# One-hot codes of a head's chosen tokens: 64 comparisons with a constant over four token tiles, where eight comparisons of two tensors stood, and the gathering put in the same order

## The reference

```python
q = jnp.einsum('bsd,hd->bhs', x, Wq)
keys = jnp.einsum('bsd,hd->bhs', x, Wk)
v = jnp.einsum('bsd,ed->bse', x, Wv).reshape(B, S, H, dv).transpose(0, 2, 1, 3)
k_idx = jnp.argsort(keys, axis=-1)
k_sorted = jnp.take_along_axis(keys, k_idx, axis=-1)
v_sorted = jnp.take_along_axis(v, k_idx[..., None], axis=2)
top_keys, bot_keys = k_sorted[:, :, -k:], k_sorted[:, :, :k]      # k = 32
top_vals, bot_vals = v_sorted[:, :, -k:, :], v_sorted[:, :, :k, :]
attn_top = jax.nn.softmax(q[..., None] * top_keys[:, :, None, :], axis=-1)
attn_bot = jax.nn.softmax(q[..., None] * bot_keys[:, :, None, :], axis=-1)
...
out = q_pos * out_top + (1.0 - q_pos) * out_bot
```

## Time and profile before

| | |
|---|---|
| median of 3 runs | 1083.82 us (1082.76 to 1086.74) |
| the profiled execution | 1083.07 us |
| its span, first to last instruction | 1080.8 us |
| mean granted TensorE clock | 0.924 of full speed |
| busy: TensorE, VectorE, ScalarE, GpSimd | 903.8, 880.1, 620.6, 457.1 us |
| the one-hot operations (L1950) | 16 of them, 40.5 us in all |
| the attention of the second block | about 733 to 966 us of the span |

### The profile page before, as it was taken

How to read it: one execution, slowest core, us unless ns; L and a number is a source line. 1 busy time by engine, 2 the same in 40 slices (tenths; PEclk the granted TensorE clock), 3 DMA queues, 4 the chain that set the end, 5 groups by cost and what they waited for, 6 DMA issues and landing times. The chain is left out here.

```text
span 1080.8 us, 16981 instructions
## 1 busy us (share of the span) xinstructions
PE 903.8 (84%) x5454; PEld 603.9 (56%) x5454; DVE 880.1 (81%) x1724; ACT 620.6 (57%) x1331; POOL 457.1 (42%) x439
## 2 busy tenths in 40 slices
PE   5568999999999999999889969985288558747996
PEld 4346777777777777777667725463222442234554
DVE  6868999999999999988899787669979787665443
ACT  2568777777778787777677522215268508614111
POOL 2337666777675454554445562112500410007332
PEclk9889999999999999999999989998679769956999
DMA  5013433334433222321222310001000000021001
GB/s 195 25 59 109 133 135 122 123 104 124 134 128 113 69 79 81 125 89 60 78 85 73 139 58 1 2 30 29 2 0 1 1 1 1 1 78 55 1 1 40
DMA packets 44031, 72.44 MB, mean 67 GB/s; under 512 B 4595, under 2 KB 20979, under 8 KB 43305
## 3 DMA queue, kind: packets, MB, share of 16 engines
q1 hardware_dynamic: 34728, 58.79, 17.1%
q10 hardware_dynamic: 9216, 12.59, 3.1%
HBM read 56.81 MB, written 13.76 MB: 65 GB/s over the span
## 5 line engine op out<-in xcount | busy, mean ns | idle before, releaser
L477 PE MATMUL bank<-hTs,wA 128*128 128x512 bf16 x768 | 178.2, 380 | 0.8 <-DVE u L1573 0.8
L1573 DVE SCALAR_TENSOR_TENSOR u<-bank,chn,u 128x511 f32<-128x511 f32 (+2 forms) x192 | 142.9, 744 | 9.1 <-ACT u L1071 5.6
L2103 POOL TENSOR_TENSOR xbuf<-xbuf,dec 128x384 f32<-128x384 f32 x64 | 53.4, 834 | 208.1 <-ACT xbuf L1079 168.8
L548 PE MATMUL bank<-wB,yb 128*128 128x256 f32 x512 | 121.2, 380 | 0.7 <-DVE acc L1529 0.7
L477 PEld LDWEIGHTS bank<-hTs,wA 128*128 128x128 bf16 x768 | 75.1, 98 | 83.4 <-issue 3.9
L548 PEld LDWEIGHTS bank<-wB,yb 128*128 128x128 f32 x512 | 92.5, 190 | 11.1 <-issue 1.1
L477 PE MATMUL bank<-hTs,w13s 128*128 128x512 bf16 x372 | 92.5, 396 | 7.1 <-DVE uc L1801 3.8
L2163 POOL TENSOR_TENSOR hfl<-hf 128x512 bf16<-128x512 f32 x44 | 46.0, 1044 | 120.3 <-DVE hf L1811 66.6
L2113 POOL TENSOR_TENSOR yb<-yv,gs 128x512 f32<-128x512 f32 x64 | 81.7, 1276 | 15.5 <-DVE yv L1600 15.3
L621 PE MATMUL bank<-Mm,xbuf 128*128 128x128 f32 x512 | 69.8, 279 | 21.0 <-DVE yv L1600 18.6
L1089 ACT ACTIVATE rel<-csb,cs 128x128 f32<-128x128 f32 x256 | 82.4, 415 | 0.0
(11 more groups left out here) (247 smaller groups left out, 2099.7 us busy)
## 6 DMA issues: line engine op xcount, KB each, us to landing
csb<-csd SPq DMA_DIRECT2D x64, 256.0 KB, 3.4
wA<-in_win SPq DMA_DIRECT2D x32, 256.0 KB, 4.3
wAd<-wA ACTq DMA_DIRECT2D x32, 256.0 KB, 4.2
wA<-wAd SPq DMA_DIRECT2D x32, 256.0 KB, 3.7
wB<-in_wob SPq DMA_DIRECT2D x8, 512.0 KB, 5.8
wBd<-wB ACTq DMA_DIRECT2D x32, 128.0 KB, 4.3
wB<-wBd SPq DMA_DIRECT2D x8, 512.0 KB, 5.4
CB<-in_wbc SPq DMA_DIRECT2D x2, 1024.0 KB, 9.4
```

The lines of the kernel that those rows point to most:

```text
L477: last = nc.tensor.matmul(out, wpart(a, kt), hpart(c, kt), start=n == 0, stop=n == 5)
L548: last = nc.tensor.matmul(out[:, 0:D], yb[:, HG * (k % 2) + m, t * P:(t + 1) * P], wB[:, k % 2, m, :], start=m == 0, stop=m == HG - 1)
L1573: nc.vector.scalar_tensor_tensor(out=u[:, n % 2, d:S], in0=bank[0][:, 0:S - d], scalar=chn[:, hid, 3 - d:4 - d], in1=u[:, n % 2, d:S], op0 ...
```

## The change

The tensor `iotak` and the operation that makes it are gone. The eight operations of each batch that compared two tensors become 64, one per side and place. Each compares all four token tiles of `cdT`, 512 elements a partition, with one number given in the instruction, and writes runs of four heads (8 bytes) into `OH`, with a distance of 256 bytes from one run to the next. The elements written are as many as before (32,768 a partition and batch). `a_oh` is raised once per side, not once per tile. The gathering matmuls are the same 256, but run side by side, then by group, then by token tile; a bank is full when the second side's matmuls of its four groups are done. `add_heads` of the second batch stands behind the first side.

```diff
-        iotak = sb("iotak", [P, 2, K, QG], bf16)
@@ TensorE, gathering
-                    for t in range(TB):
-                        pe.wait_ge(q["a_oh"], TB * b + t + 1)
+                    for side in range(2):
+                        pe.wait_ge(q["a_oh"], 2 * b + side + 1)
                         for n in range(NQ // 4):
                             for g4 in range(4):
-                                for side in range(2):
-                                    o = (g4 * 2 + side) * 48
+                                g = 4 * n + g4
+                                o = (g4 * 2 + side) * 48
+                                for t in range(TB):
                                     last = nc.tensor.matmul(
-                                        bank[n][:, o:o + 48], OH[:, t, side, 4 * n + g4, :],
-                                        PV[:, t, :, 16 * n + 4 * g4:16 * n + 4 * g4 + 4, :],
-                                        start=t == 0 and o == 0, stop=t == TB - 1, skip_group_check=True)
-                            if t == TB - 1:
+                                        bank[n][:, o:o + 48], OH[:, t, side, g, :],
+                                        PV[:, t, :, 4 * g:4 * g + 4, :],
+                                        start=o == 0 and t == 0, stop=t == TB - 1, skip_group_check=True)
+                            if side:
                                 last.then_inc(q["a_vw"], 1)
@@ VectorE
-                nc.vector.tensor_copy(iotak[:].rearrange("p s k h -> p (s k) h"),
-                                      cst[:, C_IOTA:C_IOTA + 2 * K].unsqueeze(2).to_broadcast([P, 2 * K, QG]))
...
-                    for t in range(TB):
-                        for side in range(2):
-                            last = nc.vector.tensor_tensor(
-                                OH[:, t, side].rearrange("p g (k h) -> p g k h", h=QG),
-                                cdT[:, t, :].rearrange("p (g h) -> p g h", h=QG).unsqueeze(2).to_broadcast([P, NQ, K, QG]),
-                                iotak[:, side].unsqueeze(1).to_broadcast([P, NQ, K, QG]), ALU.is_equal)
+                    for side in range(2):
+                        for k in range(K):
+                            last = nc.vector.tensor_scalar(OH[:, :, side, :, QG * k:QG * (k + 1)],
+                                                           cdT[:].rearrange("p t (g h) -> p t g h", h=QG),
+                                                           float(side * K + k + 1), None, ALU.is_equal)
                         last.then_inc(q["a_oh"], 1)
-                        if b and t == 0:
+                        if b and side == 0:
                             add_heads(b - 1)
```

## The result

| | median us | range | n | before beside it, us (n) | ratio to before, 95% interval |
|---|---|---|---|---|---|
| changed | 1077.79 | 1074.89 to 1080.38 | 6 | 1083.43 (6) | 0.993 [0.9912, 0.9949] |
| changed, second measurement | 1075.53 | 1073.71 to 1076.88 | 4 | 1084.32 (12) | 0.9905 [0.9886, 0.9925] |
| changed, third measurement | 1073.2 | 1070.89 to 1078.56 | 6 | 1085.0 (10) | 0.9892 [0.9861, 0.9923] |

In the third measurement one execution of before took 1152.75 us at a granted clock of 0.801 and is not counted.

A forecast was written before the change was run, and what follows sets the result against it. VectorE's one-hot codes were taken to bound the gathering and sums, in the second batch only behind `add_heads`. Gains of 3.5 + 2.0 + 0.1 = 5.6 us from 1083.07 gave 1077.5, median 1078 us; range 1075 to 1089.

The forecast's parts named there:

- The price of a comparison: On VectorE, each new 512-element comparison follows the last after 0.20 us; 0.33 or 0.60 were the alternatives.
- Rival 2: VectorE's fixed part per operation is not overlapped: pitch 0.29 us, 4.5 us slower, 1088 us; chance 0.04.
- First batch: Codes end at 779.05 instead of 783.44; sums end 4.2 or 2.8 us earlier, 3.5 taken.
- full-clock tail: From last code to end of sums, 4.5 us if TensorE gathers the second side at full clock, 5.9 at half.
- Second batch: Side 0 ends at 871.85, `add_heads` at 874.5; sums end 2.7 or 1.3 us earlier, 2.0 taken.
- the failed step: Second batch: GpSimd's last four operations alternate with one VectorE comparison each, until 868.05.
- Rival 1: VectorE handles two elements a step, not four: pitch 0.33 us, about 11 us slower, 1095 us; chance 0.13.
- Rival 3: The stream of short comparisons keeps GpSimd out until it ends, in both batches: about 1086.5 us; chance 0.05.
- The tail and the clock: Tails of 4.5 or 5.9 us behind the last codes; clock shifts in the loops behind worth 1.2 us either way.
- The sum: Gains of 3.5 us in the first batch, 2.0 in the second and 0.1 for `iotak`: 5.6 us.
- likeliest case: Whole kernel at pitch 0.20 us with turns between VectorE and GpSimd: 1075 to 1081 us; chance 0.75.

The follow-up runs named there:

- e2: Changed kernel with the copied codes `cdT` in fp32 instead of bf16: 1095.06 us, ratio to before 1.0088.
- e3: Kernel before, in its old tile-by-tile order, with 256 constant comparisons of 128 elements a batch: 1103.08 us, ratio to before 1.0169.
- e9: Changed kernel with each comparison of the second batch's side 0 cut in two of 256 elements: 1082.72 us in a single execution, before 1083.07.
- after_third: The changed kernel without edit, measured and profiled a third time: 1073.2 us, ratio to before 0.9892.
- e5: Changed kernel with the tensor `iotak` and the operation that fills it put back, unused: 1075.26 us, ratio to before 0.9909.
- e6: Changed kernel, VectorE waiting ahead of the second batch's eleventh comparison for the first of GpSimd's last four pieces: 1079.66 us, ratio to before 0.994.
- e8: Changed kernel with the ninth comparison of the second batch's side 0 reading its codes from PSUM: 1074.63 us in a single execution, before 1083.07.
- after_again: The changed kernel without edit, measured and profiled a second time: 1075.53 us, ratio to before 0.9905.
- e4: Changed kernel with the first batch's first 20 comparisons and all 32 of the second batch's side 0 reading codes from PSUM: 1074.31 us, ratio to before 0.9892.
- e7: Changed kernel with 20 comparisons of the first batch and 27 of the second batch's side 0 reading PSUM: 1072.33 us, ratio to before 0.9897.

## Why the prediction was right, and where it was not

**The price of a comparison: right.** 0.20 us was taken between 0.20, 0.33 and 0.60; 0.202 was measured. The reason holds as well (e2, e3, e9). Rival 2 is out: the pitch is 0.202 with a duration of 0.302, so the fixed part is overlapped. The Trainium skill, VectorE: DVE Perf Modes, section The DRAIN you can't avoid, which I cited for this rival, adds itself that a next operation which isn't held starts earlier; here the next one does start 0.1 us before the one ahead is over.

**First batch: the size right, the path partly by chance.** Forecast 4.2 us at the full-clock tail and 2.8 at the other, 3.5 taken; 3.9 measured from `VW` to the sums. In the runs in which VectorE reached the codes as before (22.64 us: after_third, e5, e6, e8, e9), the codes took 16.43 us, forecast 16.6 at most, and the gain is 25.80 - 21.47 = 4.3. In after_third:

```profile
765.12 16.43 DVE L1948 TENSOR_SCALAR OH<-cdT 128x512 bf16<-128x512 bf16 x64
```

In the first profile VectorE reached the codes 2.9 us earlier against its own start than before, so six of its comparisons, not three, lay beside GpSimd's operations, at 1.4 us each. What differs ahead of it is the granted clock:

```profile
724.10:737.80 13.70, 13.70 (x56) 12.16 (x54) 10.82 (x40) 0.97 (x5) 0.00 (x0) 0.50 0.18 59
```

It was 0.50 through this window in the changed kernel's profile, and 0.88 in that of before and of e5. Over the window from 715 to 745 us it is 0.77 in the five profiles with 19.6 to 20.05 us from `VW` to the codes (changed, after_again, e2, e4, e7) and 0.94 in the nine with 22.63 to 22.65. TensorE, ScalarE and with them GpSimd came later against VectorE (GpSimd's first operation of the attention starts 8.06 us behind `VW`, not 5.43), VectorE's search for keys met less of GpSimd (the two operations that write `code`, L1911 before, took 3.40 us there and 1.26 here), and its codes met more. From `VW` to the sums it hardly matters: 44.55 against 44.11 us. I call this chance and not a result of the change, because both versions occur in the same kernel (after_again and after_third) and e6 broke the only pattern.

**Second batch: the failed step.** "Then GpSimd's four last with one of VectorE behind each: 862.25 + 4 x 1.45 = 868.05", so that side 0 ends at 871.85. The prediction took the turns for a law. They hold when GpSimd is at work as VectorE's stream comes. Here the stream was running when GpSimd came, at 862.57, and its operation, 1.3 us of work, lasted 5.3 us, since it waited until the stream was over. Side 0 ended at 866.7, not 871.85, and `add_heads` at 871.4, not 874.5. Some of what this won was lost again: GpSimd's late pieces stood beside `x_sb` (2.00 us, forecast 1.24) and one comparison of side 1 (1.3 us), so side 1 took 7.58 us, not 6.4. The term of 2.0 us was really 4.8. e6 shows it from the other side: made to take turns, `add_heads` starts 13.7 us behind the copy of the codes instead of 10.1, and 1.9 us of the gain are gone. The 3.0 us that are left stand beside the forecast's 2.7 for the full-clock tail: with turns, its sum would have been about right, though e6 has a forced wait in the place of one turn.

**Rival 1: out, and its sum a little off.** Its own 112 operations at 0.133 us more, less the 5.6 of the forecast, make 9.3 us slower; it says 11. e2, which has this pitch, measured 10.7, with the sums 5.6 us later than before in the first batch (counted from `VW`) and 6.4 in the second.

**Rival 3: its mechanism came true in the second batch, and its sign was wrong.** It let GpSimd be kept out in both batches until all 64 comparisons were over and called it slower by 3 us. In the second batch GpSimd was kept out by the 32 of side 0 only: `add_heads` waits for another engine (1.37 us) and breaks the stream, and GpSimd's pieces, late by 3 us, are needed behind `add_heads` and by a gathering that ends ahead of side 1. In the first batch GpSimd had been at work first, so it was never kept out.

**The tail and the clock: right.** Both tails are those of the full clock (4.55 us), forecast 4.5 or 5.9. The low-clock stretch behind the first sums is 6.8 us instead of 9.9. From the second sums to the end of the span 191.7 us are left, 192.7 before, within the 1.2 us that the prediction gave for this.

**The sum.** Forecast 5.6 us, first comparison 5.6, but that agreement owes something to luck: the parts in the attention gained about 9, and 3.6 were lost ahead of it. The three measurements give 5.6, 8.8 and about 12 us, and the parts' 9 lies between them, so the change is probably worth more than the forecast's 5.6; the second batch's term is where it was too small. The prediction had no term for the spread of the part ahead, 6.5 us over the profiles, which is more than the 6 us of its likeliest case's whole range.

## What to carry to other kernels

Where an operation with two tensors only compares with a list of numbers, many operations with one input and a constant can be faster, if each is long enough to bury its fixed part: here 512 bf16 elements at 0.202 us won about 9 us, 128 elements at 0.102 us or 512 fp32 at 0.335 us lost 10 to 20. Where VectorE and GpSimd both work out of SBUF, ask which of them is at work first: a dense stream that is already running can keep GpSimd out to its end, while behind a working GpSimd each short operation costs a whole long one; so look at what each of the two feeds next, and put a stream ahead of the one that can wait. And cut a profile at the same events in both kernels before crediting a change with the difference of two spans: here the part ahead of the change varied by 6.5 us.

## What the runs showed of the hardware that I had not expected

- GpSimd was kept out by a stream of VectorE's operations for 4.0 us (20 comparisons of 512 bf16 elements) and for 6.2 us (about 46 of 256), in all six traces that have such a stream running when GpSimd comes (changed, after_again, after_third, e5, e8, e9). The Trainium skill, SBUF — State Buffer, section Who interferes with whom, has the first comer hold the port pair for its instruction; here GpSimd was kept out over many instructions, each of which starts 0.1 us before the one ahead of it ends. With 128 elements, or fp32, it was not, though there too the next one starts early, by 0.09 and 0.08 us.
- The same two engines in the other order (GpSimd first) take strict turns: the next pair starts 1.33 us after the last, and each of the two operations lasts 1.42 us, waiting included.
- The start of the attention, in code that no edit touches, lies between 739.0 and 745.5 us over fourteen profiles, and a stretch of 13.7 us at half clock ahead of it comes in some executions of a kernel and not in others.
